# Top-k cross-attention block on one core: Q and K levels cast on ScalarE out of PSUM, regrouping by head and all counts on ScalarE, the front one batch earlier

## What is computed

```python
for each of 32 batches, x: (256 tokens, 256), ctx: (256, 256), f32
Q = (layernorm(x) @ Wq.T + bq).reshape(16 heads, 256, 16)
K = (ctx @ Wk.T + bk).reshape(16, 256, 16)
V = (ctx @ Wv.T + bv).reshape(16, 256, 16)
scores = Q @ K.T / sqrt(16)
top 64 of the 256 scores of each row; softmax over them; their weighted sum of V rows
x = x + tanh(g_xattn) * (out @ Wo.T + bo)
x = x + tanh(g_ffn) * fp8_quantised_linear(layernorm(x))
```

## Time and profile before

| | |
|---|---|
| median of 3 runs | 3468.5 us (3457.61 to 3472.56) |
| profiled execution | 3451.94 us |
| its span, first to last instruction | 3449.7 us |
| busy DVE, ACT, PE, POOL | 88%, 67%, 53%, 28% |
| granted TensorE clock, mean | 0.711 of full speed |
| chain that ended last | DVE 56%, issue 16%, ACT 15%, PE 9% |

### The profile page before, as it was taken

How to read it: one execution, slowest core, us unless ns; L and a number is a source line. 1 busy time by engine, 2 the same in 40 slices (tenths; PEclk the granted TensorE clock), 3 DMA queues, 4 the chain that set the end, 5 groups by cost and what they waited for, 6 DMA issues and landing times.

```text
span 3449.7 us, 51070 instructions
## 1 busy us (share of the span) xinstructions
PE 1839.9 (53%) x7952; PEld 974.4 (28%) x7952; DVE 3020.4 (88%) x12951; ACT 2324.7 (67%) x8614; POOL 977.7 (28%) x1174
## 2 busy tenths in 40 slices
PE   3254455665465555464555555555455555554555
PEld 2122232332232223232222332322233222232222
DVE  2688899999899899899999999999999899998985
ACT  1775667776667766676767777776677667776771
POOL 5212223223223233222232323323223233232112
PEclk7566676667676767677767777777777767776667
DMA  4223223223323133322233322223332133332111
GB/s 72 42 32 53 47 45 56 43 46 59 50 44 56 39 52 56 53 44 45 41 58 52 60 44 53 46 46 60 50 48 53 29 60 56 53 59 31 30 23 44
DMA packets 451905, 166.47 MB, mean 48 GB/s; under 512 B 245617, under 2 KB 451441, under 8 KB 451521
## 3 DMA queue, kind: packets, MB, share of 16 engines
q1 hardware_dynamic: 451136, 162.38, 26.9%
q0 software_dynamic: 384, 0.33, 0.1%
HBM read 102.57 MB, written 59.24 MB: 47 GB/s over the span
## 4 chain that ended last, share of the span: by engine, by line
DVE 56%; issue 16%; ACT 15%; PE 9%; DVEq 2%; POOL 1%; DMA 0%; ACTq 0%; another core or an unknown queue 0%; SPq 0%; POOLq 0%
ACT act_junk L880 14%; DVE unfit L1237 9%; DVE masked L1132 6%; DVE masked L1137 6%; DVE score_sb L1033 6%; DVE following L1143 5%; PE ps_o L731 2%; PE ps_a L675 2%; DVE x_res L1293 2%; PE ps_a L684 1%; DVE above L1072 1%; DVE dve_junk L1054 1%; DVE A L1079 1%; DVE chord L1101 1%; DVE B L1080 1%
## 5 line engine op out<-in xcount | busy, mean ns | idle before, releaser
L880 ACT ACTIVATE act_junk<-score_sb,X 128x256 int8<-128x256 f32 x3840 | 1891.2, 496 | 965.3 <-DVE X L1107 429.3
L712 PE MATMUL ps_e<-qs,ks 99*128 99x256 bf16 x1024 | 346.1, 348 | 1453.7 <-DVE unfit L1237 1055.3
L731 PE MATMUL ps_o<-pT_sb,v_aug 128*32 128x256 f32 x2048 | 773.1, 518 | 0.5 <-ACT pT_sb L889 0.5
L880 ACT ACTIVATION_READ_ACCUMULATOR act_junk<-score_sb,X 128x1 f32 x3840 | 724.8, 189 | 0.0
L712 PEld LDWEIGHTS ps_e<-qs,ks 99*128 99x128 bf16 x1024 | 120.1, 117 | 1558.3 <-DVE unfit L1237 910.4
L1033 DVE TENSOR_SCALAR_CACHE_REDUCE score_sb<-ps_s 128x256 f32<-128x256 f32 x1024 | 418.2, 415 | 84.5 <-PE ps_s L698 84.2
L1237 DVE TENSOR_SCALAR unfit<-score_sb,thr 128x256 bf16<-128x256 f32 x1024 | 471.1, 482 | 9.9 <-DVE score_sb L1184 3.6
L1132 DVE TENSOR_SCALAR_CACHE_REDUCE masked<-score_sb,X 128x256 f32<-128x256 f32 x1024 | 426.3, 472 | 20.6 <-issue 8.8
L1143 DVE MAX8 following<-masked 128x8 f32<-128x256 f32 x1024 | 357.7, 409 | 1.3 <-DVE masked L1137 0.3
L716 PE MATMUL ps_e<-dropb,unfit 128*128 128x128 bf16 x2048 | 352.9, 271 | 0.0
L1137 DVE SCALAR_TENSOR_TENSOR masked<-masked,score_sb 128x1024 f32<-128x1024 f32 x256 | 325.7, 1272 | 0.1
(11 more groups left out here) (159 smaller groups left out, 3383.8 us busy)
## 6 DMA issues: line engine op xcount, KB each, us to landing
rows<-q_scr SPq DMA_DIRECT2D x192, 128.0 KB, 5.3
rows<-k_scr SPq DMA_DIRECT2D x192, 128.0 KB, 4.9
o_scr<-o_sb SPq DMA_DIRECT2D x128, 128.0 KB, 2.7
q_scr<-split SPq DMA_DIRECT2D x32, 384.0 KB, 2.7
k_scr<-split SPq DMA_DIRECT2D x32, 384.0 KB, 3.0
x_in<-in_x SPq DMA_DIRECT2D x32, 256.0 KB, 3.0
ctx_sb<-in_ctx SPq DMA_DIRECT2D x32, 256.0 KB, 2.7
v_scr<-proj SPq DMA_DIRECT2D x32, 256.0 KB, 5.8
```

What stands on the lines that cost most here:

```text
L712: nc.tensor.matmul(ps_e[:, n % 2, kc * TOK:(kc + 1) * TOK], ks[u][:, h, 8 * kc:8 * kc + 8, :].rearrange("d j t -> d (j t)"), qs[u][:, h, : ...
L731: ins = nc.tensor.matmul(ps_o[32 * c:32 * c + 32, half * TOK:(half + 1) * TOK], v_aug[p][:, 2 * h + kc, :], pT_sb[:, n % 2, kc * TOK:(kc + ...
L880: ins = nc.scalar.activation(act_junk[:, t, :], score_sb[:, slot, t, :], ACT.Sign, scale=-1.0, bias=X[slot % 2][:, 0, t:t + 1], accum_out= ...
```

## The change

- ACT counts all 16 tiles (L1054 and `s_dcnt` go).
- Biases of Q and K enter as a matmul with two rows of contraction (`qk_bias` and `blocks`), f32, 512 columns; the scale of Q goes into `wT[0]`. The projection stays in PSUM. ACT casts a level from PSUM into `split` (`keep_level`), PE subtracts that level from the same bank (`take_off`, minus the identity times the level, bf16, 512 columns), ACT casts the next: three casts each for Q and K, two subtractions each.
- `operands_by_head` is on ACT, and so is the issue of the six key loads (`load_keys`). GpSimd keeps the rest.
- The front moves ahead: in batch b, g = 1, transposes, projections and the first two levels of batch b + 3; the third level and V of batch b + 2 in g = 0 of batch b. The moments of x for batch b + 3 move from round 5 to round 1 on DVE; on GpSimd that layernorm now stands ahead of `normalise_attention`.
- The exponential lags three heads instead of four (EXP_LAG).
- Before the loop ACT runs, in order, the whole front of batches 0 and 1 with both regroupings, then the front and two levels of batch 2, and only then the first counts. On GpSimd the two `affine_select` that make `blocks` stand behind the small DMA issues, and PE waits for them before its first instruction.

```diff
+            pool.wait_ge(s_id, CONSTANTS - 2)
+            nc.gpsimd.affine_select(out=blocks[:], in_=blocks[:], compare_op=ALU.is_ge, fill=0.0, base=0,
+                                    pattern=[[1, EC * TOK]], channel_multiplier=-TOK).then_inc(s_id, 1)
...
+            def project(b):
+                pe.wait_ge(s_fe, 2 * b + 2)
+                for k, (dst, src) in enumerate(((ps_a, xT), (ps_b, cT))):
+                    nc.tensor.matmul(dst[:], qk_bias[:, k, :], blocks[:], start=True, stop=False)
...
+            def take_off(b, lev):
+                for k, dst in enumerate((ps_a, ps_b)):
+                    pe.wait_ge(s_sp, 6 * b + 2 * lev + k + 1)
+                    nc.tensor.matmul(dst[:], minusb[:], split[k][:, lev].rearrange("p c t -> p (c t)"),
+                                     start=False, stop=True, skip_group_check=True).then_inc(s_rest, 1)
...
-                            front_transposes(b + 2)
-                        if has(2) and (g, n) == (0, 4):
-                            project(b + 2, 0)
-                        if has(2) and (g, n) == (0, 6):
-                            project(b + 2, 1)
+                            project_values(b + 2)
+                        if has(3) and (g, n) == (1, 0):
+                            front_transposes(b + 3)
+                        if has(3) and (g, n) == (1, 2):
+                            project(b + 3)
+                        if has(3) and (g, n) in ((1, 5), (1, 7)):
+                            take_off(b + 3, (n - 5) // 2)
...
+            def keep_level(b, lev):
+                for k, src in enumerate((ps_a, ps_b)):
+                    if lev == 0:
+                        act.wait_ge(s_fp, 2 * b + k + 1)
+                        act.wait_ge((s_qd, s_kd)[k], at(16 * b))
+                    else:
+                        act.wait_ge(s_rest, 4 * b + 2 * (lev - 1) + k + 1)
+                    nc.scalar.copy(split[k][:, lev].rearrange("p c t -> p (c t)"), src[:]).then_inc(s_sp, 1)
+            def operands_by_head(b, u, k):
+                act.wait_ge((s_qm, s_km)[k], QK_MOVES * (b + 1))
+                act.wait_ge(s_T, at(16 * (b - OPS + 1)))
+                nc.scalar.copy((qs, ks)[k][u][0:SPLITS].rearrange("d h j t -> d j h t"),
+                               rows[:].rearrange("d j (h t) -> d j h t", t=D)).then_inc((s_qh, s_kh)[k], 1)
...
-                for t in range(ACT_TILES):
+                for t in range(GT):
...
+            for b in range(3):
                 evacuate_front(b)
+                for lev in range(2):
+                    keep_level(b, lev)
+                if b < 2:
+                    keep_level(b, 2)
+                    evacuate_values(b)
+                    operands_by_head(b, b, 0)
+                    load_keys(b)
+                    operands_by_head(b, b, 1)
...
+                            if has(2) and (g, n) == (0, 0):
+                                keep_level(b + 2, 2)
+                            if has(2) and (g, n) == (1, 1):
+                                operands_by_head(b + 2, (u + 2) % OPS, 0)
+                            if has(2) and (g, n) == (1, 2):
+                                load_keys(b + 2)
+                            if has(2) and (g, n) == (1, 5):
+                                operands_by_head(b + 2, (u + 2) % OPS, 1)
+                            if has(3) and (g, n) == (1, 1):
+                                evacuate_front(b + 3)
+                            if has(3) and (g, n) in ((1, 3), (1, 6)):
+                                keep_level(b + 3, (n - 3) // 3)
```

223 lines of the change are left out of this document (78 added, 145 removed).

## The result

| | before | after |
|---|---|---|
| median of 4 runs each, us | 3463.1 (3451.5 to 3472.6) | 3520.4 (3512.9 to 3524.9) |
| ratio, with its 95% interval | 1 | 1.0165 (1.0126 to 1.0204) |
| span of the profiled execution, us | 3449.7 | 3523.1 |
| first update of thresholds, us | 88.9 | 146.0 |
| fifth update, us | 127.4 | 185.1 |

The change makes the kernel 1.65% slower; 3545 was forecast. The difference between the two profiled executions, 73.5 us, splits in two: up to the fifth update of thresholds, the last before the batches repeat, the changed kernel loses 57.6 us, and in all that follows 15.9.

The account below looks back on a forecast made before the run. DVE was taken as the bound on average, with chain plus counts limiting some rounds. Rounds +30 us and start +51 on the median 3468.5 gave 3550, set a little lower at 3545 (+2.2%); 8-in-10 range 3415 to 3640.

Parts of the forecast that it names:

- The copy of Q in round 5, the deciding step: Round 5 on ACT: copy waits 6.0 us for the last exponents, takes 3.6, then casts and counts: 18.9 us.
- The decision point of 3.4 us: Round 5: if the copy of Q starts less than 3.4 us after L1069, the kernel is faster; that rival 0.17.
- My upper bound for the round, 20.8: Round 5: 20.8 us if the transposes run at half the speed.
- GpSimd's stalls and L1054: Removed from DVE: L1054's 0.41 us a round, stalls of 1.9 in round 4, 2.77 in round 7, 0.95 in round 1.
- that rival: Copies by head on ACT run two elements at a time: 2.0 us a batch, 60 less, 3485 us; chance 0.06.
- The start, 51 forecast: Before the loop: ACT does the fronts in series, two batches 80 us, first counts at 132, 51 later.
- two exponentials, the copy of K: Round 7 on ACT: with o_sb, less 0.25, these take 4.7 us ahead of 8.2 of counts: 12.9.
- Chain plus counts: Rounds 2 and 3: DVE's threshold chain of 3.28 us plus ACT's counts of 8.23, 11.5 each.
- 2.7 us on six DMA issues: Round 6 on ACT: six issues at SP's median of 0.45 us each, part of the round's 12.8.
- PE has room: nothing: Rounds 5 and 6: bias matmuls and subtractions add some 5 us of PE a batch, at no cost in time.
- its cover: Rounds 5 and 6: projections lie behind the copy; were that cover gone, round 6's casts would wait for the projection.
- The sum: Rounds 0 to 7: 100.2 us, 1.2 more than 99.0; over 30 batches +36, taken as +30.

Follow-up runs that it names:

- e5: The changed kernel with only the two copies by head back on GpSimd, Q's ahead of the second layernorm and K's behind it: 3557.2 us, 1.0297.
- e6: The changed kernel with ScalarE's copy of Q, key loads and copy of K each one round later: 3510.7 us, 1.0138.
- e2: The changed kernel with the next front's eight transposes one head later on TensorE, behind head 7's exponents: 3503.4 us, 1.0112.
- e4: The changed kernel with its start reordered: first counts right after V of batch 1, bias constants ahead of the small DMA issues: 3497.6 us, 1.010.
- e3: The changed kernel with the exponential again four heads behind instead of three: 3811.4 us, 1.1007.
- e9: e7 with the casts of the split moved one by one behind later counts, TensorE's steps moving with them: 3649.8 us, 1.0565.
- e7: e5 with K's copy also ahead of the second layernorm on GpSimd, and with e4's start: 3440.1 us, 0.9944.
- e12: e11 with TensorE's projection of Q at the third head of group 1 and K's at the fifth: 3336.5 us, 0.9634.
- e11: e9 with ScalarE fetching the projected values at group 0's seventh head, behind round 3's counts, not at the fifth: 3429.7 us, 0.9915.

## Why the prediction came out right, and where its steps did not

**The copy of Q in round 5, the deciding step, held.** Forecast: the copy 6.0 us after the round begins, 3.6 long, the round 18.9. Measured: 5.91, 3.60, 18.49 in batch 20, and 18.45 on average. The decision point of 3.4 us was passed by 2.5. e5 and e6 take the copy out of that place and both leave 14.2, so it costs round 5 4.3 us. e2 shows 1.4 us of its wait to be the transposes, for which I had 1.9. But the copy alone did not set the time of these rounds, as I had it: with it gone, rounds 5 and 6 together still end at 29.1 to 32.6, for 31.1. They took 24.3 before. The chain that holds them is the other one, masks, exponents, projection, casts, counts, whose length was missing from my sum. My upper bound for the round, 20.8, rested on a misreading: I took the transposes' clock from the whole of round 2 (0.78), but in their own 1.96 us, 2206.55 to 2208.51, it was 0.53, so they already ran near the lower level. In the kernel after they take 1.97.

**GpSimd's stalls and L1054 went**, as forecast. Round 4 falls by 3.5 on average, by 3.3 in batch 20, where I had 2.7; round 7 has none.

**The copy runs one element at a time.** Its 64 executions average 3605 and 3593 ns, so that rival is out. The formula of the Trainium skill (VectorE: DVE Perf Modes, "The TRN2 errata"), read with a factor of 2, gives an estimate of 1.9 us; the trace disagrees. Read with a factor of 1 the same formula gives an estimate of 3.6, which the trace bears out.

**The start, 51 forecast, 57.6 measured.** Here the size was off: two batches' fronts in series on ACT take longer than 40 us each. In the trace the first three begin at 39.87, 84.12 and 126.44, 44.3 and 42.3 apart, and the first counts start at 137.88, not 132. e4 shows that a good part of it is a matter of order: its fifth update comes 31 us earlier.

**Round 7, 12.9 forecast, 14.3 measured.** The step that failed is "two exponentials, the copy of K": the second exponential waits for a mix that waits for `o_sb`. The row at 2330.89 is that wait, 1.57 us, and the one at 2328.88 the mix's own, 1.72. e3 takes the wait away and round 7 is 12.7, so the mechanism is shown. I had read ACT's queue as if nothing in it waited, and had put no cost on the new lag of 3.

**Round 2, 11.5 forecast, 12.9 measured.** "Chain plus counts" left PE out. The projection of the values now begins in this round behind a mix, at 2267.18, and runs to 2273.5 at a granted clock of 0.50 (0.54 in the whole round); DVE's copy of scores waits 3.67 us for it. e9 moves that step away and the round is 11.65, where the prediction put it.

**Round 6, 12.8 forecast, 12.6 measured, and partly by luck.** I had ACT spend 2.7 us on six DMA issues. They cost ACT nothing: one lasted 0.31 and five 0.47, and they ran beside five counts and an exponential; the issue at 2315.07 lies under the count at 2315.06, and the counts kept their spacing of 0.49. Without them the sum would have been DVE's chain and the counts, 11.5, and batch 20 has 11.44. The average is 12.6 because of a cost that I left out: the step "PE has room: nothing" failed. On average the projection ends at 21.6, 1.4 before round 6's counts, with an exponential and the casts to come, so it ties with the copy's chain. The prediction said that if its cover were gone, the casts would wait for it; in e2, e3, e5, e6 and e7 they do (round 6's counts start 0.5 to 1.0 us behind the projection's end).

**The sum.** Batch 20 takes 100.48 where I had 100.2. Over the whole span the rounds lose 15.9 us, not 30, and the start 57.6, not 51: 73.5 together for 81. The total was better than its parts, and in that it was lucky: the rounds lost half of what was forecast and the start 13% more. Batches 4 to 28 lose 25 us, and what follows the fifth update in batches 0 to 3 is 7 shorter than before, which the prediction had in no term. And in batch 20 rounds 2 and 7 were forecast 3.4 us too short together, and rounds 1, 4, 5 and 6 2.9 too long.

**Which parts of the change cost, then.** The start, of which e4 has back 31 of 58 us by its order, and e12, with the copies on GpSimd as well, 47. The copies by head on ACT: e7, whose copies are on GpSimd with K's ahead of the layernorm, is 57 us below e4, which has nearly the same start and the copies on ACT, and only 10 of that lie up to the fifth update. In e5's order, with K's copy behind the layernorm, the gain is lost: it is 37 us slower than the change though its fifth update comes 25 earlier. Then ACT's two casts of the high level right behind the projection and ahead of round 6's counts, and the projection in one piece, which the kernel before had in two. The casts from PSUM and TensorE's removal of levels stay in e12, which is 3.7% faster than before. Two things are open: a version of e12 whose copy of Q begins behind the masks of round 5, which would avoid the stall, wasn't tried, and neither was the split of the projection on the changed kernel by itself.

## What to carry to other kernels

Moving work off the busiest engine helps only as far as no other engine takes over a wait with it: a copy that waits is cheap on an idle engine and dear in a queue whose next item is on the critical path, unless, as here, the idle engine's copy stalls another. Where two chains end within a microsecond, taking one away shows only the other, so cost each of them before deciding which is the bound. Where a long piece of matmuls stands in one engine's list ahead of short ones that others wait for, cut it in pieces that fit between them: here that alone was worth 93 us, on top of e11.

## What the hardware showed beyond what I expected

- DMA issues on ScalarE's queue ran beside running activations: of the six in batch 20, 0.31 to 0.47 us each, five lay under counts of 0.50 and one under an exponential.
- TensorE's granted clock took two values, 0.50 and 1.00, and the projection's eight matmuls took 3.78 us at the lower (e7) and 1.99 at the higher (after); the mixes 1.92 and 1.05. In e7 it fell while TensorE stood idle for 5.82 us, and was still at the lower level at 2253.2, when TensorE had been busy since 2237.09. In the kernel after it was low from 2310.9 to 2314.2 and high from 2314.4, inside one busy stretch. Over a whole span the mean clock is 0.68 in the kernel after and 0.71 in before, e7 and e12.
- GpSimd's copy of Q and DVE hindered each other in every one of the 25 batches of e5 and of e7 to e12. Where DVE's long two-input instruction or its count began behind the copy, it ended only behind it (2.7 to 4.7 us for 1.22 or 0.48). Where the copy began while the long instruction ran, the copy took 4.3 to 4.7 us for 3.59, and the pair of masks that came next took 2.29 for 0.60.
